# One Mamba-2 layer on one core: squares folded on GpSimd, the loop written out, new orders on every engine

## What is computed

```python
xn = layernorm(x)
z, xBC, dt = split(xn @ W_in)                # 512, 768, 8 columns
dt = softplus(dt + dt_bias)
X, B, C = split(silu(causal_conv(xBC)))      # 512, 128, 128; 4 taps
y = ssd(X * dt, dt * a, B, C) + X * D        # 8 heads of 64, state 128
y = y * silu(z)
y = y * rsqrt(mean(y * y) + EPS) * rms_w     # the squares of this change
h = xn + y @ W_out
out = x + layernorm(h) * ln_g + ln_b + tanh(xn @ W1 @ W2 @ W3 + bias)
```

## Time and profile before

| | us |
|---|---|
| median of 3 runs | 767.18 (766.02 to 770.41) |
| the profiled execution | 769.67 |
| its span in the trace | 768.0 |
| mean granted clock of TensorE | 0.981 |

### The profile page before, as it was taken

One profiled execution on the slowest core, in us unless ns is written; L12 is line 12 of the kernel. 1 busy time (PEld: TensorE's weight loads), 2 busy tenths in 40 slices (PEclk: granted clock), 3 DMA queues, 4 the chain that ended last, 5 costly groups with the idle time before them and its releaser, 6 DMA issues. The chain is left out here.

```text
span 768.0 us, 17761 instructions
## 1 busy us (share of the span) xinstructions
PE 712.0 (93%) x4728; PEld 574.9 (75%) x4728; DVE 686.3 (89%) x1321; ACT 580.4 (76%) x1425; POOL 597.5 (78%) x932
## 2 busy tenths in 40 slices
PE   5979999999999989998999989999999999999983
PEld 4767777787778677786887768777787878877763
DVE  3779999898989879898998989989899999989884
ACT  3787878877797777876878678787878778787851
POOL 2538798787978769886897968879787888979773
PEclk7999999999999999999999999999999999999996
DMA  6001310211212021120211212011121202011110
GB/s 214 2 4 32 97 56 18 85 31 31 70 46 71 19 65 48 30 69 19 82 31 30 69 46 68 18 58 55 31 71 45 72 18 72 16 32 56 32 56 29
DMA packets 60073, 38.35 MB, mean 50 GB/s; under 512 B 7120, under 2 KB 59472, under 8 KB 59984
## 3 DMA queue, kind: packets, MB, share of 16 engines
q1 hardware_dynamic: 58768, 37.40, 16.0%
q10 hardware_dynamic: 1216, 0.02, 0.1%
HBM read 27.70 MB, written 8.65 MB: 47 GB/s over the span
## 5 line engine op out<-in xcount | busy, mean ns | idle before, releaser
L2626 PE MATMUL ring<-xhl,wh 128*128 128x512 f32 x620 | 207.8, 416 | 1.4 <-DVE xs L1136 1.2
L1136 DVE SCALAR_TENSOR_TENSOR xs<-ring,cw,xs 128x512 f32<-128x512 f32 x273 | 196.6, 738 | 6.3 <-issue 5.0
L2626 PEld LDWEIGHTS ring<-xhl,wh 128*128 128x128 f32 x620 | 107.5, 189 | 33.1 <-issue 11.2
L2157 ACT ACTIVATE xdt<-xt_bank,dts 128x64 f32<-128x64 f32 x512 | 111.8, 334 | 13.8 <-PE xt_bank L2712 13.5
L2626 PE MATMUL ring<-xhl,wl 128*128 128x512 f32 x310 | 122.0, 394 | 0.0
L634 POOL TENSOR_TENSOR lay<-lay,xd 128x512 f32<-128x512 f32 x62 | 79.9, 1288 | 31.3 <-DVE lay L1174 31.3
L2087 ACT ACTIVATE xs<-ring,cb,cw 128x512 f32<-128x512 f32 x91 | 71.9, 790 | 38.8 <-PE ring L2626 38.3
L1165 DVE SCALAR_TENSOR_TENSOR lay<-e_bank,btg 128x512 f32<-128x512 f32 x128 | 85.4, 678 | 0.0
L2137 ACT ACTIVATE e_bank<-e_bank 128x512 f32<-128x512 f32 x128 | 76.0, 605 | 7.5 <-PE e_bank L2742 7.3
L2626 PE MATMUL bg_bank<-woh,yts 128*128 128x256 f32 x252 | 74.9, 297 | 5.6 <-DVE hh L1239 4.3
L627 POOL TENSOR_TENSOR xd<-xs,d_ch 128x512 f32<-128x512 f32 x64 | 67.1, 1048 | 14.4 <-ACT xs L2102 13.2
(11 more groups left out here) (184 smaller groups left out, 1838.5 us busy)
## 6 DMA issues: line engine op xcount, KB each, us to landing
grow<-scratch SPq DMA_DIRECT2D x124, 128.0 KB, 3.0
xin<-in_x_dram SPq DMA_DIRECT2D x32, 256.0 KB, 2.8
out_dram<-res SPq DMA_DIRECT2D x31, 256.0 KB, 2.6
right<-rows SPq DMA_DIRECT2D x256, 2.0 KB
left<-rows SPq DMA_DIRECT2D x256, 2.0 KB
lay<-in_w_in_dram SPq DMA_DIRECT2D x1, 776.0 KB, 8.6
lay<-in_w_in_dram SPq DMA_DIRECT2D x1, 512.0 KB, 10.2
sq<-in_w_out_dram SPq DMA_DIRECT2D x1, 512.0 KB, 5.4
```

Of the source, the lines that this page charges most:

```text
L1136: v.scalar_tensor_tensor(out=to, in0=conv_bank(j, ct), scalar=cw[:, ct, t:t + 1], in1=to, op0=ALU.mult, op1=ALU.add).then_inc(tap_done[ct], 1)
L2157: last = s.activation(xdt[:, q, head], xt_bank[:, head], ACT.Copy, scale=dts[:, b, at:at + 1])
L2626: last = mul(out, a, c, start=first and i == 0, stop=i == n - 1)
```

## The change

1. `fold` moves from DVE to POOL: in place of a reduction of 4 blocks to 1, one addition of blocks 0 and 1 to blocks 2 and 3, which leaves 2 blocks of 128 tokens. `folded` has twice the size, and `square_sum` issues two products that accumulate, where it had one.
2. The hardware loop over steps 4 to 11 is a loop of the generating program: the eight passes are written out, and their waits and addresses are constants.
3. The orders of `head`, `one_pass` and `tail` are new on SP, POOL, DVE, ACT and PE. `one_pass` also begins at another point of a step on each of them.

```diff
-        folded = sb("folded", [P, Q, P])
+        folded = sb("folded", [P, Q, 2, P])
...
-            with eng.Fori(first // BUF, last // BUF) as i:
+            for i in range(first // BUF, last // BUF):
                 for b in range(BUF):
                     one_pass(i * BUF + b, b, 1 - b)
...
 @block.gpsimd
+            def fold(j, b, c, q):
+                k = C * j + c
+                pool.wait_ge(sq_done[q], k + 1)
+                if begun(k - 1):
+                    pool.wait_ge(ss_in_psum, Q * k)
+                g.tensor_tensor(folded[:, q], sq[:, q, 0:2], sq[:, q, 2:4], ALU.add).then_inc(folded_done[q], 1)
...
 @block.vector
-            def fold(j, b, c, q):
-                k = C * j + c
-                dve.wait_ge(sq_done[q], k + 1)
-                if begun(k - 1):
-                    dve.wait_ge(ss_in_psum, Q * k)
-                v.tensor_reduce(folded[:, q], sq[:, q].rearrange("p k t -> p t k"), AXIS.X, ALU.add).then_inc(folded_done[q], 1)
...
 @block.tensor, square_sum
-                mul(ss_bank[:, q], folded[:, q], ones[:, 0:2], start=True, stop=True).then_inc(ss_in_psum, 1)
+                mul(ss_bank[:, q], folded[:, q, 0], ones[:, 0:2], start=True, stop=False)
+                mul(ss_bank[:, q], folded[:, q, 1], ones[:, 0:2], start=False, stop=True).then_inc(ss_in_psum, 1)
```

Of the new orders, those that the prediction speaks of. A pass on SP:

```diff
             def one_pass(j, b, b1):
+                load_again(j + 1, b1, 1)
                 spread_growth(j - 1, b1, 0, 0)
+                spread_factors(j - 1, b1, 1)
                 spread_growth(j - 1, b1, 0, 1)
-                spread_factors(j - 1, b1, 1)
                 spread_growth(j - 1, b1, 1, 0)
                 store(j - 2, b, 0)
+                load_again(j + 2, b, 0)
+                store(j - 2, b, 1)
+                put_growth(j, b)
                 spread_growth(j - 1, b1, 1, 1)
-                store(j - 2, b, 1)
-                load_again(j + 2, b, 0)
-                load_again(j + 2, b, 1)
-                put_growth(j, b)
                 spread_factors(j, b, 0)
```

The beginning of the heads of DVE, ACT and PE (`negate_a` needs ACT's `exp_a`, and that the loads of `a_log`):

```diff
 DVE             norm_stats(0, 0, 1)
+                negate_a()
                 norm_mean_var(0, 0)
...
 ACT             first_table()
+                exp_a()
                 conv_high(0)
                 f_inner_out(0)
+                conv_high(1)
+                f_inner_out(1)
                 norm_apply(0, 0, 0)
                 norm_apply(0, 0, 1)
-                conv_high(1)
-                f_inner_out(1)
...
 PE              f_inner()
+                f_outer()
                 transpose_x(0, 0, 0)
                 transpose_x(0, 0, 1)
-                f_outer()
+                branch_project(0, 0, 0, 0)
+                branch_project(0, 0, 0, 1)
+                conv_project(0, 0, 3)
                 conv_project(0, 0, 2)
```

More of the change, by code:

```diff
@@ new lines, in head @@
+                softplus(3, 1, 0)
+                scale_x(2, 0, 1, 0)
+                softplus(3, 1, 1)
+                fold(2, 0, 0, 1)
+                softplus(3, 1, 2)
+                mask_g(2, 0, 1, 1)
+                softplus(3, 1, 3)
+                softplus(3, 1, 4)
+                softplus(3, 1, 5)
+                softplus(3, 1, 6)
+                softplus(3, 1, 7)
+                join_skip(2, 0, 1, 0)
+                softplus(3, 1, 8)
+                rms_scale(2, 0, 0)
+                softplus(3, 1, 9)
@@ new lines, in one_pass @@
+                tap(j - 1, b1, 1, 0)
+                tap(j - 1, b1, 3, 2)
+                tap(j - 1, b1, 1, 1)
+                scale_off(j - 2, b, 1, 0)
+                mean_square(j - 2, b, 0)
+                weigh(j - 2, b, 1, 1, 0)
+                join_spill(j - 1, b1, 1)
+                tap(j - 1, b1, 4, 0)
+                y_low(j - 2, b, 0, 1)
+                tap(j - 1, b1, 0, 0)
+                tap(j - 1, b1, 1, 2)
+                last_h(j - 2, b, 0, 0)
+                add_diag(j - 2, b, 1, 0)
@@ L1456, in head @@
-                last_h(0, 0, 0, 0)
-                tap(1, 1, 0, 2)
-                tap(1, 1, 1, 0)
-                new_state(0, 0, 1, 0)
-                tap(1, 1, 1, 1)
+                tap(1, 1, 3, 1)
+                tap(1, 1, 3, 2)
+                tap(1, 1, 1, 0)
+                add_diag(0, 0, 0, 1)
+                join_spill(1, 1, 1)
+                scale_off(0, 0, 1, 0)
+                apply_gate(0, 0, 0, 1)
+                weigh(0, 0, 1, 0, 0)
+                tap(1, 1, 0, 0)
+                tap(1, 1, 1, 1)
@@ new lines, in head @@
+                tap(1, 1, 0, 1)
+                y_low(0, 0, 0, 1)
+                norm_stats(2, 0, 0)
+                mean_square(0, 0, 0)
+                tap(1, 1, 0, 2)
+                tap(1, 1, 1, 2)
+                weigh(0, 0, 1, 0, 1)
+                new_state(0, 0, 1, 0)
+                join_spill(1, 1, 0)
+                tap(1, 1, 4, 0)
+                last_h(0, 0, 0, 0)
+                tap(1, 1, 4, 1)
+                scale_off(0, 0, 1, 1)
+                tap(1, 1, 5, 0)
+                last_stats(0, 0, 0, 0)
@@ L1684, in tail @@
                 tap(12, 0, 1, 1)
+                scale_off(11, 1, 1, 0)
+                mean_square(11, 1, 0)
+                weigh(11, 1, 1, 1, 0)
                 join_spill(12, 0, 1)
-                mean_square(11, 1, 0)
+                tap(12, 0, 4, 0)
+                y_low(11, 1, 0, 1)
+                tap(12, 0, 0, 0)
+                tap(12, 0, 1, 2)
+                last_h(11, 1, 0, 0)
                 add_diag(11, 1, 1, 0)
-                tap(12, 0, 4, 0)
+                tap(12, 0, 0, 1)
@@ L1760, in tail @@
                 tap(13, 1, 1, 1)
+                scale_off(12, 0, 1, 0)
+                mean_square(12, 0, 0)
+                weigh(12, 0, 1, 1, 0)
                 join_spill(13, 1, 1)
-                mean_square(12, 0, 0)
+                tap(13, 1, 4, 0)
+                y_low(12, 0, 0, 1)
+                tap(13, 1, 0, 0)
+                tap(13, 1, 1, 2)
+                last_h(12, 0, 0, 0)
                 add_diag(12, 0, 1, 0)
-                tap(13, 1, 4, 0)
+                tap(13, 1, 0, 1)
@@ L1836, in tail @@
                 tap(14, 0, 1, 1)
+                scale_off(13, 1, 1, 0)
+                mean_square(13, 1, 0)
+                weigh(13, 1, 1, 1, 0)
                 join_spill(14, 0, 1)
[L1838 removed]
+                tap(14, 0, 4, 0)
+                y_low(13, 1, 0, 1)
+                tap(14, 0, 0, 0)
+                tap(14, 0, 1, 2)
+                last_h(13, 1, 0, 0)
                 add_diag(13, 1, 1, 0)
[L1840 removed]
+                tap(14, 0, 0, 1)
```

1926 lines of the change are left out of this document (924 added, 1002 removed).

## The result

| | before | after |
|---|---|---|
| median, runs on one chip (us) | 766.61 (766.02 to 770.41, 4 runs) | 803.08 (802.11 to 806.79, 4 runs) |
| ratio of the times | | 1.047 (95%: 1.043 to 1.051) |
| profiled execution, its span | 769.67, 768.0 | 806.79, 805.1 |

The account below looks back on a forecast made before the run. PE and DVE were taken to set the pace. The terms summed as 769.67 −15.1 −15.4 +2.5 −1.0 = 740.7, and 2.5 less for the median gave 738.2, stated as 739 us; range 724 to 757, eight times in ten.

Parts of the forecast that it names:

- Part 1: Loop over steps 4 to 11 written out: eight stretches fall from 367.1 to 352.0 us, −15.1.
- Fetching at nothing: Instruction fetching for the longer written-out code was priced at zero; its bound was the whole 15.1 us.
- rival 4: Written-out code stalls on fetching, the 15.1 us come back, 753 us; its chance lies within that of Rival 1.
- Part 3: New orders: SP's moves cost nothing, the first 40 us cost +2.5 us, the end after the last `sums` gives −1.
- Part 2: Fold to POOL: DVE loses 4.2 us a step, POOL gains 2.9, TensorE 0.6; gain 1.1 a step.
- 0.1 a step taken for contention: Cost in us of DVE's `join_spill` meeting POOL's folds on SBUF; at most 2.2 a step.
- term of −15.4: Gain from moving the fold: 1.1 us a step on 14 stretches from step 1 to step 15.
- Rival 1: Only the loop counts; PE sets the pace and four folds fewer on DVE move nothing; 754.6 us, chance 0.20.
- Rival 3: POOL becomes the bound, keeping its waits and adding the folds: 47.0 us a step, 788 us, chance 0.07.
- term of +2.5: Cost in us of the new orders in the first 40 us, from a later `negate_a` and first product.
- the drain: After the last `sums`, where PE waits for folds: −1 us from shorter folds on POOL and a shorter last step.

Follow-up runs that it names:

- e3: Kernel before the change with its hardware loop alone written out, orders and fold as before; 754.80 us, ratio 0.980.
- f1: Changed kernel, orders untouched, the small factor transfers on SP joined in pairs, 8 a chunk in place of 16; 745.74 us, ratio 0.970.
- f2: e3 with the factor transfers on SP joined in the same pairs; 743.17 us, ratio 0.967.
- e1: Changed kernel with `spread_growth` of (chunk 0, q 1) put back ahead of `spread_factors` of chunk 1 on SP; 778.79 us, ratio 1.012.
- e4: e3 with `spread_factors` of chunk 1 put ahead of `spread_growth` of (chunk 0, q 1), as in the changed kernel; 816.81 us, ratio 1.062.
- e2: e1 with, besides, the load of the next step's second half moved ahead of chunk 0's factors on SP; 792.68 us, ratio 1.029.
- g3: f2 with the fold kept on DVE but made as two additions in place of the reduction; 769.55 us, ratio 1.002.
- g1: e1 with factor transfers joined in pairs and the second product of `square_sum` left out, so half the squares are missing; 741.76 us, ratio 0.965.

## Why the prediction was wrong

**Part 1, the loop written out: right.** −15.1 was forecast, −15.2 measured (e3). The nearness to a tenth is luck: the eight stretches took 353.0 (352.0 forecast, 367.1 before), which is 14.1, and 1.1 came off in steps whose code had not changed. Fetching at nothing held too, so rival 4 falls: e3's steps are 44.1.

**Part 3 is where it failed.** The step reads: "`spread_factors` and `put_growth` move by a place or two; what waits for their data, `exponents` and `scale_off`, comes later in the order than they do: nothing", and of the load "half a pass ahead of its `norm_stats`: nothing". I compared places in two orders and never put times to them. A place on SP is not a unit: `spread_factors` is one name and 16 issues, 10 us, and the growth of (0, 1) was moved behind it. The data came "in order" and about 4 us late, on a transfer whose landing decides when the step can close. The count of 16 stood in my own description of the kernel; I priced no issue on SP at all. Worked out, it would have been: `sums` + 1.7 (growth put) + 16 x 0.62 for chunk 0 + load and `spread_growth` (0, 0) + 16 x 0.62 for chunk 1 = 26 us, and some 3 more to land, in a step of 44 in which `scale_off` (0, 1) wants it at 25.8.

The loss can be followed through the runs. The loop gave −15.2 (e3). From e3 to the changed kernel it is +48.3 by the times, 52 by the ratios. With short queues on both sides the same pair differs by +2.6 (f1, f2). So about 46 of the 48 pass through SP's issuing; in them is the lower clock, some 5 us in the steps from 4 on, which falls away with the short queue as well. Of these the one exchange carries 24 in the new orders (e1), and 62 in the old (e4), where nothing else was arranged for it. The rest is the load and the store held behind factors; that both waits are there in e1, and that both go with the short queue, is shown, how the remaining 22 divide between them is not: e2, which was to separate the load, only moved the wait on to the factors.

**Part 2, the fold: the prices right, the gain not there.** The addition took 735 ns (737 forecast, by the line between 461 and 1288), POOL's work came to 40.2 a step (40.5), the second product cost 0.06 us a call (0.15). DVE came to 38.9 in f1 and not 37.5: its busy time fell by 2.8 a step where the fold's leaving should have taken 4.2. Of the 1.4 missing, the port has 0.6: `join_spill` takes 22.7 us in 48 calls in f1 and 13.3 in f2, and its median in the changed kernel is 532 ns where it was 186. So the 0.1 a step taken for contention was a sixth of what came, inside its bounds of 0.1 and 2.2. For the other 0.8 I have no row: the mean of no other group of DVE rose by as much as 1%, but durations in the trace overlap their neighbours' by up to a tenth of a microsecond, and a busy time is their union. The rule of the Trainium skill ("SBUF — State Buffer", Who interferes with whom), that a DVE instruction with two SBUF inputs and a GpSimd instruction that reads SBUF exclude each other, agrees with all of this, g3 most of all, and so does its remark that a reduction on trn2 does not contend: the reduction kept its time, 956 to 1093 ns over the 64 of f2, and the two additions did not keep theirs.

The term of −15.4 failed for another reason. "The busiest of the engines with trustworthy records stood 2.3 us under the pace", I wrote of DVE, and subtracted as if DVE set it. f2 shows the same DVE at 41.7 in a step of 43.5, f1 one of 38.9 in 43.8, with PE 43.0 and 43.7 busy. In f1 PE has 82% of the chain that ended last; in f2 it has 42% and DVE 26%, so DVE was on the path there, and yet taking 2.8 us off it, with PE's work as it was (g1), moved the step by 0.1. Rival 1 had the mechanism, that four folds fewer on DVE move nothing. Between steps of 44.1 (e3) and 43.5 (f2) lay waits on SP, not DVE's work.

**Rival 3, POOL as the bound, gave nearly the right size (788) for a reason that didn't occur.** Its sum was wrong besides: 767.18 + 22 + 1.5 is 791, and the 2.5 down to the median had been taken off twice. f1 has the same POOL work in steps of 43.8. What I had written as its mark, PE waiting for `folded` or `a_all` in each step, isn't among the changed kernel's long waits; `scale_off`'s is.

**The ends.** `sums` of step 1 came 2.2 us later (+2.5 forecast) and `negate_a` at 10.42 (10.3):

```profile
10.42 0.17 DVE L1306 TENSOR_SCALAR a_neg<-a_neg 128x16 f32<-128x16 f32 x1 [4.12 <-ACT a_neg L2016]
```

The way to the 2.2 was otherwise than worked out: the first product of step 0 starts at 22.17, not 24.4, only 0.75 later than before. The rest belongs to SP again: with joined transfers `sums` of step 1 comes at 71.89 (f1), 1.4 earlier than in the kernel before. The term of +2.5 came out near by accident. For the drain −1 was forecast and +4.9 measured; in f1, with the short queue, it is 56.8 us long, 1.8 less than before.

## What to carry to other kernels

Treat the queue that issues DMAs as an engine: give each operation its count of issues times the measured time of one, lay them end to end from the instant that their data exist, and compare with when the consumer wants them; "before it in the order" is no such comparison. If a queue is full for half a step behind the point that starts it, cut the number of transfers before reordering them: joining pairs was worth 57 us here where the best exchange gave 24 and the next one cost 14. And when work moves off an engine, check first that this engine, and not the one beside it at 98%, sets the pace.

## What the runs showed of the hardware that I had not expected

A DMA of a few rows holds SP's queue 0.62 us from start to start, and in f1 one that moves twice the rows 0.68 us, so for such small ones the number of transfers counts far more than what they carry. Two of DVE's additions with both operands in SBUF, beside a GpSimd that is busy 84% of a step, went from 370 and 291 ns to up to 1149 and 1259. A wait of PE of about 3 us behind the late `scale_off` was followed at once, in three of eleven steps of the changed kernel and nine of eleven of e4, by 3 to 4 us at the lower clock, and the step became about 1 us longer by it. And the hardware loop's eight steps gave back 14.1 us of the 15.1 that its seams and waits had shown.
